# Attention on one core: fewer accumulating transfers in the softmax denominators, and their sums two key tiles earlier

## The chip, the cores and the metric

The kernel runs on one core of one Trainium2 chip. The metric is the device time of one execution in microseconds (us). The engines of the core are named as the profile names them: PE is TensorE (matmuls) and PEld its weight loads, DVE is VectorE, ACT is ScalarE, POOL is GpSimd, SP is SyncE, which here only issues transfers.

## What is computed

The reference is one transformer block, conditioned on a second input: batch 2, 2048 positions, width 512, 16 heads of 32, all in fp32.

```
h = _rmsnorm(x, g1) * (1.0 + scale1[:, None, :]) + shift1[:, None, :]
x = x + _mha(h, w_qkv, b_qkv, w_ao, b_ao, n_head)
h = _rmsnorm(x, g2) * (1.0 + scale2[:, None, :]) + shift2[:, None, :]
x = x + _ffn(h, w_fc, b_fc, w_fo, b_fo)

# in _mha:
attn = jnp.einsum('bhqd,bhkd->bhqk', q, k) * (1.0 / np.sqrt(hd))
attn = jax.nn.softmax(attn, axis=-1)
out = jnp.einsum('bhqk,bhkd->bhqd', attn, v)
```

The change touches only the softmax's denominators: for each head and query, the sum of the exponentials over all 2048 keys.

## The kernel before

Four stages follow each other: the weights' preparation, the projections of queries, keys and values (stage A), attention (stage B, `stage_b`), and the output projection with the feed-forward part. Stage B is where the change is.

Stage B works through 32 units. A unit is one group of 4 heads of one batch with one block of 512 queries; four units in a row share a group of heads, so keys and values are loaded once in four units. A unit has 16 key tiles (`NK`) of 128 keys, called kt 0 to 15. For each key tile and head TensorE makes a 128x512 block of scores (line 840, tile b_s, three banks used in turn), ScalarE exponentiates it into `pt` (line 696), and TensorE multiplies it with the values into b_o (line 895). `pt` is a ring of 8 slots, one key tile each with all 4 heads: key tile kt + 8 overwrites the slot of key tile kt. TensorE works two key tiles at a time: 16 matmuls of scores and of maxima (the next units' maxima, line 812, read by VectorE at line 756) and then the products of both key tiles, one group of 16 records at line 895. Scores run 3 blocks ahead of the products.

The denominators are made by two engines and the transfer engines. In unit u GpSimd first adds key tiles 0 and 1 into the accumulator `acc` (`first_pair`, line 719). Each other pair of key tiles, n = 0 to 6 for the key tiles 2n + 2 and 2n + 3, is first folded by an accumulating transfer of 1 MB, which adds the even slot into the odd one inside `pt` (`fold_pair`, line 726); it may start when the products of both have been made. Then GpSimd adds the odd slot into `acc` (`add_pair`, line 733). The slot of an even key tile is free for ScalarE when its transfer has landed, that of an odd one when its add is done; `slot_free` holds these waits. GpSimd has one instruction stream, written out by hand: while the transfer of pair n flies it adds pair n - 1. The last pair's add of unit u stands in unit u + 1, behind the first fold. When all of a unit's adds are done, four matmuls with a column of ones (`denominators`, line 819) sum `acc` over the partitions; they stand behind the products of key tile 7 of the next unit (`D_AT`), and ScalarE copies them out (line 668) at the place that `SUMS_AT` sets. SP issues, per unit, the loads of queries (768 KB), the store of the output (256 KB), small transfers for maxima and denominators, and in three of four units two or three loads of 512 KB of the next group's keys and values (`load_piece`; none from unit 28 on): one when the products of key tile 2 are done, one behind key tile 5, one behind the maxima.

Of the kernel before, what the change touches and what calls it, by code (L numbers as in the profile page):

```python
# [17 lines left out]
ALU = mybir.AluOpType  # L18
# [4 lines left out]
HD = D // H  # L23
# [6 lines left out]
GH = P // HD  # L30
NG = NB * H // GH
NK = T // P
UNITS = NG * NJ
# [438 lines left out]

PAIRS = NK // 2 - 1
ADDS = PAIRS + 1
RING = 8
LEAD = 3
EARLY = 4
TURN_AT = 3  # L480
SUMS_AT = 4 * 8 + LEAD


def score_place(i):

    return i + (i >= SUMS_AT)

# [6 lines left out]
def stage_b(nc, io, keep, scratch):  # L494
# [9 lines left out]
    with ExitStack() as stack:  # L504
        m = Memory(nc, stack, "b")
        ident, ones = keep["ident"], keep["ones"]
# [4 lines left out]
        pt = m.sb("pt", [P, RING, GH, TB])  # L511
        acc = [m.sb(f"acc{i}", [P, GH, TB]) for i in range(2)]
# [7 lines left out]
        ps_s, ps_m, ps_o = m.ps("s", LEAD), m.ps("m", EARLY), m.ps("o", 1)  # L520
        k_in, v_in, m_in = ([m.sem(f"{n}{i}") for i in range(2)] for n in ("k_in", "v_in", "m_in"))
        q_in = [m.sem(f"q_in{i}") for i in range(4)]
        pair_in = [m.sem(f"pair_in{i}") for i in range(2)]
# [13 lines left out]
        PER = ITEMS // NK  # L537
        AHEAD = PER * (NK - TURN)
        assert all(o.count("m") == PER and o.count("s") == GH for o in ORDER)
        D_AT = 7  # L540
        assert SUMS_AT == GH * (D_AT + 1) + LEAD

        def added(u, n):

            return ADDS * u + ADDS + (n + 3 if n < PAIRS - 1 else 2 + ADDS)

        STEPS = GH * NK
        assert ITEMS == STEPS
# [9 lines left out]
        def run(eng, body):  # L558
            for u in range(UNITS):
                body(u, u // 8, u % 8)  # L560
# [93 lines left out]
        @block.scalar  # L654
        def _(act):
            act.sem_inc(p_ready, STEPS)
            act.sem_inc(d_read, 1)

            def read_products(u):

                act.wait_ge(pv_done, NK * u + RING - 1)
                act.wait_ge(o_stored, 16 * (u + 1))
                act.activation(o_sb[:], ps_o[:, 0, :], ACT.Copy).then_inc(o_read, 1)

            def read_denominators(u):
                act.wait_ge(d_ps, u + 1 + 1)
                act.wait_ge(d_out, 16 * (u + 1))
                act.activation(d_sb[:], ps_s[:, SUMS_AT % LEAD, :], ACT.Copy).then_inc(d_read, 1)

            def slot_free(u, kt, pair, j):  # L670

                act.wait_ge(pv_done, NK * u + kt + 1)
                old = (kt - RING) % NK
                if old >= 2 and old % 2 == 0:
                    g = PAIRS * (j if kt >= RING else j - 1) + old // 2 - 1
                    if g >= 0:
                        act.wait_ge(pair_in[g % 2], 16 * (PAIRS * 4 * pair + g // 2 + 1 + g % 2))
                    else:
                        act.wait_ge(pool_added, added(u - 1, old // 2 - 1))
                elif old >= 2:  # L680
                    act.wait_ge(pool_added, added(u if kt >= RING else u - 1, old // 2 - 1))
                else:
                    act.wait_ge(pool_added, ADDS * u + ADDS + 1)

            act.wait_ge(ones_ready, 3)
            act.wait_ge(o_init, 1)

            def body(u, pair, j):
                for kt in range(NK):
                    slot_free(u, kt, pair, j)  # L690
                    for h in range(GH):
                        i = GH * kt + h
                        if i == SUMS_AT:
                            read_denominators(u)
                        act.wait_ge(st_done, STEPS * (u + 1) + i + 1)
                        act.activation(pt[:, kt % RING, h, :], ps_s[:, score_place(i) % LEAD, :], ACT.Exp,  # L696
                                       scale=SCALE).then_inc(p_ready, 1)
                        if i == GH:
                            read_products(u)

            run(act, body)
            read_products(UNITS)
            read_denominators(UNITS)

        @block.gpsimd
        def _(pool):
            pool.memset(one_rows, 1.0).then_inc(ones_ready, 1)
            pool.memset(acc[1][:], 1.0).then_inc(ones_ready, 1)
            pool.wait_ge(ones_in, 32)
            pool.memset(pt[:, RING - 2:RING, :, :], 1.0).then_inc(ones_ready, 1)  # L710
            pool.wait_ge(ones_ready, 3)
            pool.dma_start(pt[:, RING - 1, :, :], pt[:, RING - 2, :, :], accum_op=ALU.add).then_inc(pair_in[1], 16)
            pool.sem_inc(pool_added, ADDS)

            def first_pair(u, slot):

                pool.wait_ge(p_ready, STEPS * (u + 1) + GH * 2)
                pool.wait_ge(d_ps, u + 1)
                pool.tensor_tensor(acc[slot][:], pt[:, 0, :, :], pt[:, 1, :, :], ALU.add).then_inc(pool_added, 1)

            def fold_pair(u, j, pair, n):

                kt = 2 * n + 3
                pool.wait_ge(pv_done, NK * u + RING - 1 + kt + 1)
                pool.nop(nofuse=True)
                pool.dma_start(pt[:, kt % RING, :, :], pt[:, (kt - 1) % RING, :, :], accum_op=ALU.add).then_inc(pair_in[(PAIRS * j + n) % 2], 16)  # L726

            def add_pair(u, j, pair, n, slot):

                g = PAIRS * j + n  # L730
                pool.wait_ge(pair_in[g % 2], 16 * (PAIRS * 4 * pair + g // 2 + 1 + g % 2))
                pool.wait_ge(pool_added, added(u, n) - 1)
                pool.tensor_tensor(acc[slot][:], acc[slot][:], pt[:, (2 * n + 3) % RING, :, :], ALU.add).then_inc(pool_added, 1)  # L733

            def body(u, pair, j):
                first_pair(u, j % 2)
                fold_pair(u, j, pair, 0)
                add_pair(u - 1, j - 1, pair, PAIRS - 1, (j + 1) % 2)
                for n in range(1, PAIRS):
                    fold_pair(u, j, pair, n)  # L740
                    add_pair(u, j, pair, n - 1, j % 2)

            run(pool, body)
            pool.sem_inc(pool_added, 1)
            add_pair(UNITS - 1, 7, UNITS // 8 - 1, PAIRS - 1, 1)

        @block.vector
# [49 lines left out]
        def _(pe):  # L797
# [17 lines left out]
            def denominators(u, slot):  # L815

                pe.wait_ge(pool_added, added(u - 1, PAIRS - 1))
                for h in range(GH):
                    last = pe.matmul(ps_s[h * HD:(h + 1) * HD, SUMS_AT % LEAD, :], ones[:, 0:HD], acc[slot][:, h, :], start=True, stop=True)
                last.then_inc(d_ps, 1)  # L820

            def operands(j, pair):
# [8 lines left out]
            def scores(n, kslot, qslot, i):  # L831

                kt, h = i // GH, i % GH
                place = score_place(i)
                if place == SUMS_AT + LEAD:
                    pe.wait_ge(d_read, n + 2)
# [6 lines left out]
            for i in range(SUB):  # L843
                last = pe.matmul(ps_o[:, 0, i * P:(i + 1) * P], ones[:], ones[:], start=True, stop=True)
# [13 lines left out]
            def body(u, pair, j):  # L858
# [4 lines left out]
                for kt in range(NK):  # L863
# [28 lines left out]
                    for n in (kt - 1, kt):  # L892
# [4 lines left out]
                        last.then_inc(pv_done, 1)  # L897
                    if kt == D_AT:
                        pe.wait_ge(p_ready, STEPS * (u + 1) + SUMS_AT - LEAD + 1)
                        denominators(u, (j + 1) % 2)  # L900

            run(pe, body)
            denominators(UNITS, 1)


# [480 lines left out]
def build(nc, io, out):  # L1386

    scratch = {}
    for name, shape in (("qk_hi", (2, NG, P, T)), ("qk_lo", (2, NG, P, T)), ("v", (NG, P, NK, P)), ("o", (NG, P, T)),
                        ("h_hi", (NG, P, T)), ("h_lo", (NG, P, T)),   # L1390
                        ("y1", (NB, T, D)), ("m", (2, 2, GH * TB)), ("d", (GH, TB)), ("r", (NG, GH, T))):
        scratch[name] = nc.dram_tensor(f"scratch_{name}", shape, F32, kind="Internal").ap()
    with ExitStack() as whole:
        m = Memory(nc, whole, "keep")
        keep = {"chan": m.sb("chan", [P, C_ALL]), "cond_ab": m.sb("cond_ab", [P, NB, 4, KT]),
                "ident": m.sb("ident", [P, P]), "ones": m.sb("ones", [P, P]),
                "w_ao": m.both("w_ao", [P, KT, D])}
        with ExitStack() as early:
            m = Memory(nc, early, "early")
            keep |= {"w_hi": m.sb("w_hi", [P, KT, 3 * D], F32R), "w_lo": m.sb("w_lo", [P, KT, 3 * D], F32R),  # L1400
                     "cos": m.sb("cos", [P, T]), "sin": m.sb("sin", [P, T]), "bv": m.sb("bv", [P, D]),
                     "x": m.sb("x", [P, SUB, D])}
            stage_p(nc, io, keep)
            stage_a(nc, io, keep, scratch)
        nc.disable_value_cache = True
        stage_b(nc, io, keep, scratch)
        nc.disable_value_cache = False
        stage_cd(nc, io, keep, scratch, out)
# [43 lines left out]
```

## Time and profile before

| | us |
|---|---|
| median of 3 runs | 3324.93 (3324.06 to 3326.23) |
| profiled execution, its own time | 3321.67 |
| its span in the trace | 3319.9 |
| stage B from the first to the last regular group of sums | 508.02 to 2012.39 |

The span is from the first to the last instruction in the trace; the execution's own time is 1.8 us longer. Stage B has 33 groups of sums at line 819 (one for each unit and one of the start), and the distance from one to the next is the length of a unit. A unit is named below by the start of the group of sums that opens it.

### The profile page before, as it was taken

To read this page: it belongs to the slowest core of one execution; us is meant where nothing else is said; L and a number is where in the kernel's file an instruction comes from. 1 tells how busy PE (TensorE), PEld (TensorE's weight loads), DVE (VectorE), ACT (ScalarE), POOL (GpSimd) and SP (SyncE) were. 2 spreads that over 40 slices of the span, in tenths; PEclk is the share of its full clock that TensorE was granted. 3 is DMA by queue.
4 is the path that set the end of the run, shared out by engine and by line. 5 is a ranking of instruction groups with operands and counts; after the bars stand their busy time and mean duration, and the time that the engine had idled before them with its cause. 6 is when DMAs were issued, how large, how long until landed. Compare 5 with 4: busy or idle time off the path is not lost. (4 is left out here: it accounts for less than half of the span.)

```text
span 3319.9 us, 41114 instructions
## 1 busy us (share of the span) xinstructions
PE 3118.5 (94%) x15089; PEld 2089.3 (63%) x15089; DVE 1839.2 (55%) x2971; ACT 1513.8 (46%) x2790; POOL 1719.3 (52%) x748
## 2 busy tenths in 40 slices
PE   5999789999999999999999999399999999999999
PEld 5777545555555555555555553177888888888887
DVE  2566478787777787777887882153333333222222
ACT  1323117776666676676776776242222223111111
POOL 0445518888888888888888888432222310000000
PEclk9999859999999999999999999699999999999999
DMA  4454539899898998889999887522222211112110
GB/s 181 142 162 154 150 79 201 188 196 189 184 197 180 198 192 176 195 175 199 191 189 197 174 174 158 137 89 88 85 82 76 84 37 58 51 66 87 51 51 26
DMA packets 168670, 455.25 MB, mean 137 GB/s; under 512 B 23961, under 2 KB 57833, under 8 KB 135789
## 3 DMA queue, kind: packets, MB, share of 16 engines
q0 software_dynamic: 32400, 235.94, 35.6%
q1 hardware_dynamic: 134800, 211.01, 21.6%
q10 hardware_dynamic: 1296, 6.03, 0.5%
q8 instruction: 104, 1.70, 0.2%
q14 instruction: 70, 0.57, 0.1%
HBM read 137.94 MB, written 78.92 MB: 65 GB/s over the span
## 5 line engine op out<-in xcount | busy, mean ns | idle before, releaser
L756 DVE TENSOR_REDUCE b_mpart<-b_m 128x1 f32<-128x512 f32 x2048 | 1253.1, 681 | 342.4 <-PE b_m L812 341.8
L696 ACT ACTIVATE b_pt<-b_s 128x512 f32<-128x512 f32 x2048 | 1085.7, 603 | 418.5 <-PE b_s L840 358.5
L733 POOL TENSOR_TENSOR b_acc<-b_acc,b_pt 128x2048 f32<-128x2048 f32 x225 | 1045.9, 4648 | 207.8 <-DMA b_pt<-b_pt 205.4
L840 PE MATMUL b_s<-b_qs,b_ks 98*128 98x512 f32 x2048 | 856.7, 421 | 39.4 <-ACT b_pt L696 32.4
L812 PE MATMUL b_m<-b_ks,b_qs 96*128 96x512 f32 x2048 | 811.1, 423 | 20.3 <-issue 20.1
L840 PEld LDWEIGHTS b_s<-b_qs,b_ks 98*128 98x128 f32 x2048 | 390.0, 191 | 376.5 <-issue 183.6
L812 PEld LDWEIGHTS b_m<-b_ks,b_qs 96*128 96x128 f32 x2048 | 399.8, 195 | 173.0 <-DVE b_mpart L756 81.1
L895 PE MATMUL b_o<-b_pt,b_vg 128*32 128x512 f32 x4096 | 505.0, 611 | 0.0
L1212 DVE SCALAR_TENSOR_TENSOR e_u_lo_f<-e_a,keep_chan,e_u_lo_f 128x512 f32<-128x512 f32 x128 | 96.1, 751 | 547.9 <-PE e_a L1333 547.9
L1106 ACT ACTIVATE e_u_lo_f<-e_g,keep_chan 128x512 f32<-128x512 f32 x128 | 88.3, 690 | 423.6 <-PE e_g L1333 423.5
L895 PEld LDWEIGHTS b_o<-b_pt,b_vg 128*32 128x32 f32 x4096 | 108.5, 111 | 249.8 <-ACT b_pt L696 137.6
L1111 ACT ACTIVATE e_u_hi<-e_u_lo_f 128x512 fp32r<-128x512 f32 x128 | 81.0, 633 | 344.4 <-DVE e_u_lo_f L1212 344.4
L726 POOL DMA_DIRECT2D b_pt<-b_pt x224 | 204.6, 913 | 39.8 <-PE b_o L895 28.0
L1333 PE MATMUL e_g<-e_h_hi,e_w_hi 128*128 128x512 f32 x512 | 200.9, 392 | 13.1 <-DVE e_h_lo L1233 13.1
L1333 PE MATMUL e_a<-e_h_hi,e_w_hi 128*128 128x512 f32 x512 | 200.7, 392 | 0.0
L1343 PE MATMUL e_y<-e_w_hi,e_u_hi 128*128 128x512 f32 x512 | 200.7, 392 | 0.0
L1333 PE MATMUL e_g<-e_h_lo,e_w_hi 128*128 128x512 f32 x512 | 199.8, 390 | 0.0
L1333 PE MATMUL e_g<-e_h_hi,e_w_lo 128*128 128x512 f32 x512 | 199.8, 390 | 0.0
L1333 PE MATMUL e_a<-e_h_hi,e_w_lo 128*128 128x512 f32 x512 | 199.8, 390 | 0.0
L1343 PE MATMUL e_y<-e_w_hi,e_u_lo 128*128 128x512 f32 x512 | 199.7, 390 | 0.0
L1333 PE MATMUL e_a<-e_h_lo,e_w_hi 128*128 128x512 f32 x512 | 199.5, 390 | 0.0
L1343 PE MATMUL e_y<-e_w_lo,e_u_hi 128*128 128x512 f32 x512 | 199.5, 390 | 0.0
(140 smaller groups left out, 3300.3 us busy)
## 6 DMA issues: line engine op xcount, KB each, us to landing
b_pt<-b_pt POOLq DMA_DIRECT2D x225, 1024.0 KB, 8.2
scratch_qk_hi<-a_q_hi SPq DMA_DIRECT2D x64, 256.0 KB
scratch_qk_lo<-a_q_lo SPq DMA_DIRECT2D x64, 256.0 KB
b_qs<-scratch_qk_hi SPq DMA_DIRECT2D x64, 256.0 KB, 5.9
b_ks<-scratch_qk_hi SPq DMA_DIRECT2D x32, 512.0 KB, 7.0
scratch_o<-b_o_sb SPq DMA_DIRECT2D x33, 256.0 KB, 8.7
early_x<-in_x SPq DMA_DIRECT2D x8, 1024.0 KB, 8.2
scratch_v<-a_vsb SPq DMA_DIRECT2D x32, 256.0 KB, 4.4
```

The source lines that it names most:

```text
L696: act.activation(pt[:, kt % RING, h, :], ps_s[:, score_place(i) % LEAD, :], ACT.Exp, scale=SCALE).then_inc(p_ready, 1)
L726: pool.dma_start(pt[:, kt % RING, :, :], pt[:, (kt - 1) % RING, :, :], accum_op=ALU.add).then_inc(pair_in[(PAIRS * j + n) % 2], 16)
L733: pool.tensor_tensor(acc[slot][:], acc[slot][:], pt[:, (2 * n + 3) % RING, :, :], ALU.add).then_inc(pool_added, 1)
L756: dve.tensor_reduce(mpart[j % 2][:, i // 4, i % 4:i % 4 + 1], ps_m[:, at, :], AX.X, ALU.max).then_inc(max_done, 1)
L812: pe.matmul(ps_m[:, maximum_bank(j, place), :], qs[qslot][0:KR, h, s * P:(s + 1) * P], ks[kslot][0:KR, h, k * TB:(k + 1) * TB], start=True ...
L840: pe.matmul(ps_s[:, place % LEAD, :], ks[kslot][0:QR, h, kt * P:(kt + 1) * P], qs[qslot][0:QR, h, :], start=True, stop=True).then_inc(st_d ...
L895: last = pe.matmul(ps_o[h * HD:(h + 1) * HD, 0, :], vg[kslot][:, n, h * HD:(h + 1) * HD], pt[:, n % RING, h, :], start=n == 0, stop=n == N ...
L1106: act.activation(u_f[:, f % 2, :], ps_g[:, 0, :], ACT.Silu, bias=chan[:, t:t + 1]).then_inc(sg_ready, 1)
L1111: act.activation(u_hi[:, f % 2, :], u_f[:, f % 2, :], ACT.Copy).then_inc(uhi_ready, 1)
L1212: dve.scalar_tensor_tensor(u, ps_a[:, 0, :], chan[:, t:t + 1], u, ALU.add, ALU.mult).then_inc(uf_ready, 1)
L1333: last = pe.matmul(ps[:, 0, :], w[:, f, t, k, :], h[s][:, k, :], start=i == 0, stop=i == 3 * KT - 1)
L1343: last = pe.matmul(ps_y[:, i, :], u[:, f % 2, i * P:(i + 1) * P], w[:, f, :], start=f == 0 and n == 0, stop=f == NF - 1 and n == 2)
```

## The change

The last pair of a unit, key tiles 14 and 15, is no longer folded by a transfer. Key tile 14 is added by GpSimd straight from its slot (`add_single`), and key tile 15 by TensorE: the sums over the partitions take a second term, four more matmuls that read its slot and accumulate in the same bank. So a unit has six pairs (`PAIRS`) and six transfers, and still eight adds on GpSimd. The add of the last pair (key tiles 12 and 13) and the single add now stand ahead of `first_pair` of the next unit. The sums move from behind key tile 7 to behind key tile 5. The waits of the ring follow: the slot of key tile 14 waits for the single add, that of key tile 15 for the sums.

```
-PAIRS = NK // 2 - 1
-ADDS = PAIRS + 1
+PAIRS = NK // 2 - 2
+ADDS = PAIRS + 2
-SUMS_AT = 4 * 8 + LEAD
+SUMS_AT = 4 * 6 + LEAD
...
-        D_AT = 7
+        D_AT = 5
...
-            return ADDS * u + ADDS + (n + 3 if n < PAIRS - 1 else 2 + ADDS)
+            return ADDS * u + ADDS + (n + 4 if n < PAIRS - 1 else 2 + ADDS)
...
                 old = (kt - RING) % NK
-                if old >= 2 and old % 2 == 0:
+                if old == NK - 1:
+                    act.wait_ge(d_ps, u + 1 + 1)
+                elif old == NK - 2:
+                    act.wait_ge(pool_added, ADDS * u + ADDS + 1)
+                elif old >= 2 and old % 2 == 0:
...
-                else:
-                    act.wait_ge(pool_added, ADDS * u + ADDS + 1)
+                elif kt >= RING:
+                    act.wait_ge(pool_added, ADDS * u + ADDS + 3)
...
+            def add_single(u, slot):
+
+                pool.wait_ge(p_ready, STEPS * (u + 1) + GH * (NK - 1))
+                pool.wait_ge(pool_added, added(u, PAIRS - 2))
+                pool.tensor_tensor(acc[slot][:], acc[slot][:], pt[:, (NK - 2) % RING, :, :], ALU.add).then_inc(pool_added, 1)
+
             def body(u, pair, j):
+                add_single(u - 1, (j + 1) % 2)
+                add_pair(u - 1, j - 1, pair, PAIRS - 1, (j + 1) % 2)
                 first_pair(u, j % 2)
                 fold_pair(u, j, pair, 0)
-                add_pair(u - 1, j - 1, pair, PAIRS - 1, (j + 1) % 2)
                 for n in range(1, PAIRS):
                     fold_pair(u, j, pair, n)
                     add_pair(u, j, pair, n - 1, j % 2)
...
             def denominators(u, slot):
 
                 pe.wait_ge(pool_added, added(u - 1, PAIRS - 1))
-                for h in range(GH):
-                    last = pe.matmul(ps_s[h * HD:(h + 1) * HD, SUMS_AT % LEAD, :], ones[:, 0:HD], acc[slot][:, h, :], start=True, stop=True)
+                pe.wait_ge(p_ready, STEPS * (u + 1))
+                terms = [acc[slot][:]] + [pt[:, n % RING, :, :] for n in (NK - 1,)]
+                for n, term in enumerate(terms):
+                    for h in range(GH):
+                        last = pe.matmul(ps_s[h * HD:(h + 1) * HD, SUMS_AT % LEAD, :], ones[:, 0:HD], term[:, h, :],
+                                         start=n == 0, stop=n == len(terms) - 1)
                 last.then_inc(d_ps, 1)
```

GpSimd's stream around a unit's start, before: `first_pair` is line 719, the DMA rows are folds, and line 733 is `add_pair`. The piece runs from the last fold of a unit through the first two adds of the next.

```order
L726 DMA b_pt<-b_pt 128x2048
L733 TENSOR_TENSOR b_acc<-b_acc,b_pt 128x2048
L719 TENSOR_TENSOR b_acc<-b_pt 128x2048
L726 DMA b_pt<-b_pt 128x2048
L733 TENSOR_TENSOR b_acc<-b_acc,b_pt 128x2048
L726 DMA b_pt<-b_pt 128x2048
L733 TENSOR_TENSOR b_acc<-b_acc,b_pt 128x2048
```

The same place of the changed kernel, where line 730 is the fold, 737 `add_pair`, 743 `add_single` and 723 `first_pair`.

```order
L730 DMA b_pt<-b_pt 128x2048
L737 TENSOR_TENSOR b_acc<-b_acc,b_pt 128x2048
L743 TENSOR_TENSOR b_acc<-b_acc,b_pt 128x2048
L737 TENSOR_TENSOR b_acc<-b_acc,b_pt 128x2048
L723 TENSOR_TENSOR b_acc<-b_pt 128x2048
L730 DMA b_pt<-b_pt 128x2048 x2
L737 TENSOR_TENSOR b_acc<-b_acc,b_pt 128x2048
```

Ahead of `first_pair` there are now three adds in a row, and behind it two folds in a row with no add between them; before, the previous unit's last add stood between these two folds.

TensorE's stream at the sums of a unit, before, from the last products ahead of them.

```order
L895 MATMUL b_o<-b_pt,b_vg 32x512 x8
L819 MATMUL b_s<-b_acc,keep_ones 32x512 x4
L840 MATMUL b_s<-b_qs,b_ks 128x512
L812 MATMUL b_m<-b_ks,b_qs 128x512
```

And of the changed kernel, where it stands one group of products earlier (line 833 is the sums, 855 the scores, 823 the maxima, 910 the products).

```order
L910 MATMUL b_o<-b_pt,b_vg 32x512 x8
L833 MATMUL b_s<-b_acc,keep_ones 32x512 x4
L833 MATMUL b_s<-b_pt,keep_ones 32x512 x4
L855 MATMUL b_s<-b_qs,b_ks 128x512
L823 MATMUL b_m<-b_ks,b_qs 128x512
```

## Rows read from the trace of the kernel before

**Rows 1.** The page: busy time by engine, and slices of the span.
```profile
PE 3118.5 (94%) x15089; PEld 2089.3 (63%) x15089; DVE 1839.2 (55%) x2971; ACT 1513.8 (46%) x2790; POOL 1719.3 (52%) x748
...
POOL 0445518888888888888888888432222310000000
...
DMA  4454539899898998889999887522222211112110
```

**Rows 2.** Windows: stretch, length, busy us of PE, PEld, DVE, ACT, POOL, clock, DMA share, GB/s.
```profile
508.02:2012.39 1504.37, 1470.42 (x7954) 790.63 (x7950) 1196.03 (x2040) 1045.93 (x1980) 1273.91 (x451) 0.99 0.90 188
...
1058.46:1106.89 48.43, 48.35 (x269) 26.25 (x265) 39.80 (x68) 34.84 (x66) 42.13 (x16) 1.00 0.90 188
1106.89:1160.54 53.65, 50.26 (x270) 26.50 (x266) 40.08 (x68) 34.92 (x66) 42.32 (x16) 0.97 0.95 196
```

**Rows 3.** Waits of ACT between 556.5 and 2012.4: total, times, longest.
```profile
ACT b_pt L696 <- POOL b_acc L733: 39.8, 17, 4.4
ACT b_pt L696 <- DMA b_pt<-b_pt: 9.6, 7, 3.1
```

**Rows 4.** Timeline of PE around the sums, and one unit's products.
```profile
1058.46 1.04 PE L819 MATMUL b_s<-b_acc,keep_ones 128*32 128x512 f32 x8
1059.43 0.50 PE L840 MATMUL b_s<-b_qs,b_ks 98*128 98x512 f32 x1
...
1093.49 1.92 PE L895 MATMUL b_o<-b_pt,b_vg 128*32 128x512 f32 x16
...
1099.31 1.92 PE L895 MATMUL b_o<-b_pt,b_vg 128*32 128x512 f32 x16
...
1105.15 1.92 PE L895 MATMUL b_o<-b_pt,b_vg 128*32 128x512 f32 x16
```

**Rows 5.** Timeline of POOL, an undisturbed unit.
```profile
1042.26 4.59 POOL L719 TENSOR_TENSOR b_acc<-b_pt 128x2048 f32<-128x2048 f32 x1
1047.57 0.87 POOL L726 DMA_DIRECT2D b_pt<-b_pt  x1 [0.73 <-PE b_o L895]
1048.18 4.86 POOL L733 TENSOR_TENSOR b_acc<-b_acc,b_pt 128x2048 f32<-128x2048 f32 x1
1053.38 0.87 POOL L726 DMA_DIRECT2D b_pt<-b_pt  x1 [0.33 <-POOL b_acc L733]
1054.62 4.58 POOL L733 TENSOR_TENSOR b_acc<-b_acc,b_pt 128x2048 f32<-128x2048 f32 x1 [0.37 <-DMA b_pt<-b_pt]
...
1072.24 0.87 POOL L726 DMA_DIRECT2D b_pt<-b_pt  x1 [0.83 <-PE b_o L895]
...
1080.01 4.57 POOL L733 TENSOR_TENSOR b_acc<-b_acc,b_pt 128x2048 f32<-128x2048 f32 x1 [1.07 <-DMA b_pt<-b_pt]
```

**Rows 6.** Timeline of POOL, the next unit, with loads of keys.
```profile
1101.81 0.88 POOL L726 DMA_DIRECT2D b_pt<-b_pt  x1 [0.32 <-POOL b_acc L733]
...
1112.26 4.59 POOL L733 TENSOR_TENSOR b_acc<-b_acc,b_pt 128x2048 f32<-128x2048 f32 x1 [3.18 <-DMA b_pt<-b_pt]
...
1122.27 0.87 POOL L726 DMA_DIRECT2D b_pt<-b_pt  x1
...
1132.09 4.59 POOL L733 TENSOR_TENSOR b_acc<-b_acc,b_pt 128x2048 f32<-128x2048 f32 x1 [0.96 <-PE b_o L895]
```

**Rows 7.** Timeline of ACT: exponentials of an undisturbed unit, then of the disturbed one.
```profile
1053.27 4.24 ACT L696 ACTIVATE b_pt<-b_s 128x512 f32<-128x512 f32 x8 [1.58 <-PE b_s L840]
...
1150.10 2.06 ACT L696 ACTIVATE b_pt<-b_s 128x512 f32<-128x512 f32 x4 [3.07 <-DMA b_pt<-b_pt]
1154.73 3.26 ACT L696 ACTIVATE b_pt<-b_s 128x512 f32<-128x512 f32 x6 [2.56 <-POOL b_acc L733]
```

**Rows 8.** All folds (L726) between 556.5 and 2012.4.
```profile
DMA to landing us min/median/max: 6.9/8.3/13.4
```

**Rows 9.** Timeline of POOL, last unit: its first fold and its last add.
```profile
2050.88 0.87 POOL L726 DMA_DIRECT2D b_pt<-b_pt  x1 [1.43 <-PE b_o L895]
...
2093.96 4.49 POOL L733 TENSOR_TENSOR b_acc<-b_acc,b_pt 128x2048 f32<-128x2048 f32 x1 [1.49 <-DMA b_pt<-b_pt]
```

More of the change, by code:

```diff
@@ L709, in _ @@
             pool.wait_ge(ones_in, 32)
-            pool.memset(pt[:, RING - 2:RING, :, :], 1.0).then_inc(ones_ready, 1)
+            pool.memset(pt[:, RING - 4:RING, :, :], 1.0).then_inc(ones_ready, 1)
             pool.wait_ge(ones_ready, 3)
-            pool.dma_start(pt[:, RING - 1, :, :], pt[:, RING - 2, :, :], accum_op=ALU.add).then_inc(pair_in[1], 16)
+            pool.dma_start(pt[:, RING - 3, :, :], pt[:, RING - 4, :, :], accum_op=ALU.add).then_inc(pair_in[1], 16)
             pool.sem_inc(pool_added, ADDS)
@@ L743, in _ @@
             run(pool, body)
-            pool.sem_inc(pool_added, 1)
+            add_single(UNITS - 1, 1)
             add_pair(UNITS - 1, 7, UNITS // 8 - 1, PAIRS - 1, 1)
```

## The prediction, made before the changed kernel had run

> **What bounds the kernel now.** I read the page's busy times and slices first. TensorE is busy 94% of the span, and GpSimd, busy over half of it, has its work in stage B alone, where the transfer engines run at 8 to 9 tenths as well [rows 1]. So stage B has three nearly full resources, and the average doesn't say which one ends a unit. The windows do. The 30 units from 508.02 to 2012.39 took 1504.37 us, 50.15 each, but an undisturbed one takes 48.43 us with PE busy for 48.35 and a clock of 1.00, and a disturbed one 53.65 at 0.97 [rows 2]. The floor of a unit is thus TensorE's 48.43 us, and 1504.37 - 30 x 48.43 = 51.5 us are stalls on top.
>
> The waits name their cause: ScalarE waited 39.8 us for GpSimd's adds and 9.6 us for the accumulating transfers, 49.4 us together [rows 3], always for a slot of the ring. In the disturbed unit both stand next to each other [rows 7]: the transfer and the add of the unit's last pair were late, and with the exponentials the scores, since TensorE has three banks for them.
>
> **GpSimd's chain.** Call the start of a unit's first products 0. From the sums at 1058.46, which follow the start of the products of key tile 7 by 1.74 us (1105.15 to 1106.89), and from groups 5.83 us apart [rows 2, 4], the undisturbed unit has its 0 at 1039.23 and the next at 1087.66. A fold starts 2.5 us behind its group of products (1053.38 against 1050.88). An add takes 4.58 us, the next add starts 0.6 us behind a fold's issue (1047.57 to 1048.18), and the first transfer's add starts 7.05 us after its issue, the fifth's 7.77 [rows 5]. Call that time D. The last pair's add ends at 1053.04, and key tile 7's first exponential, second in the batch of 1053.27, starts at 1053.87 [rows 5, 7]: 0.8 us in hand. With loads beside them D is longer: 10.45 for the second transfer, 9.82 for the fifth [rows 6]; the median to landing is 8.3, the shortest 6.9 [rows 8].
>
> When GpSimd is late and no product holds a fold back, fold n + 2 follows add n, and add n waits for landing n. Its unit is then a loop through every second transfer: D, add 0 (fold 2 follows), D, add 2, D, add 4, then fold 6's issue, add 5 and the next first_pair. That is 3D + 3 x 4.58 + 0.6 + 4.58 + 4.59 = 3D + 23.5. At D = 8.3 it is 48.4, the very floor of TensorE. This explains why some units stall and some don't.
>
> **The change, part by part.**
>
> TensorE. Four more matmuls with the column of ones, of the same shape as those at line 819, which took 1.04 us, the next instruction starting 0.97 us after them [rows 4]. I take 0.97; half a group of products (1.92 for eight) gives 0.96, so no range is needed. All of it lies on TensorE, which nothing covers in an undisturbed unit: the floor becomes 49.40 us. Over 32 units that is +31 us. Moving the sums two key tiles up costs nothing by itself: what they wait for, the last add of the unit before, comes earlier too (below). The new wait for exponentials of the unit before is long fulfilled, and ScalarE's wait for the sums before it writes key tile 7 stands right behind its own copy of these sums.
>
> Transfers. One of seven goes, 1 MB of some 9 MB a unit. GpSimd saves its issue (0.87, of which 0.6 lay in the loop). Its adds stay eight: the single add takes the place of the seventh pair's.
>
> GpSimd's order. The loop is now D, add 0, D, add 2, D, add 4, single add, add 5, first_pair: 3D + 5 x 4.58 + 4.59 = 3D + 27.5, four us more for the same D. The reason: before, the last add of the previous unit stood between folds 0 and 1, inside the first flight; now the two folds stand next to each other, and GpSimd has nothing to do until transfer 0 has landed, 6 us or more. The second fold can't help, as it also waits for the products of key tile 5 (11.65 + 2.5 = 14.15). The loop equals the floor of 49.40 only at D = 7.3, against 8.3 before.
>
> What is due when. The last transferred pair is key tiles 12 and 13, and key tile 5 overwrites slot 13. This exponential lies as far behind the products of key tile 3 as key tile 7's did behind those of key tile 5 (1053.87 - 1050.88 = 3.0): 5.83 + 3.0 = 8.8. In an undisturbed unit fold 4 starts 1087.66 - 1072.24 = 15.4 us before the next 0, its add after 7.77, and three adds end at -15.4 + 7.8 + 13.7 = 6.1. So 2.7 us are in hand where 0.8 were. But they are in hand once: with D above 7.3 each unit eats 3 x (D - 7.3), and none gives back, since even undisturbed transfers are near 7.3.
>
> Which D. It can't be below 6.9, the shortest seen, and has little reason to lie above 8.3, the median with a seventh transfer in the way. For relief: the seventh transfer flew beside the query loads into the next unit's first. Against: when GpSimd is late, folds 0 and 1 go out at 13 to 14, just as SP's load behind key tile 5 does in three of four units; that load now strikes transfer 0, which is in the loop, and not transfer 1 alone. The load behind the maxima still meets transfers 3 and 4. With 8.5, 7.4 and 8.1 for transfers 0, 2 and 4 I take a mean D of 8.0: a loop of 51.5 us, 2.1 above the floor, in the 28 units that have or follow such loads.
>
> In sentences of its own, a page's price: the Trainium skill, DMA: Bandwidth & Descriptors, Anatomy of one DMA, gives a transfer from GpSimd 2.0 us plus its bytes over 436 GB/s, an estimate of 4.4 us for 1 MB. By it the loop would be 40.7 us and TensorE would bind every unit. The rows show no landing below 6.9 for these accumulating transfers, so I go by the rows.
>
> The sum: TensorE +31; the old stalls, -51.5; the new ones, 28 x 2.1 less the 2.7 in hand, +56; the end of the last unit, where TensorE is done and only the chain counts: before 47.6 us from its first fold to the end of its last add (2050.88 to 2098.45 [rows 9]), now 3 x 7.3 + 5 x 4.58 = 44.8, -3. Together +32.5. The longer filling of two more slots at the start lies ahead of the first exponential and has no reader that waits. The profiled execution took 3321.67, giving 3354; the median of the runs is 3.3 above it, giving 3358.
>
> **The rivals.**
>
> No stalls at all (0.20). One transfer less and the queries' loads falling between units bring D to 7.3 or less; the 2.7 us in hand take up the rest. For it: D was 7.05 where nothing else flew. Against: the loads haven't changed. It gives +31 - 51.5 - 3 = -23.5, 3301. This is the case on the other side; it decides from D = 7.3.
>
> Break-even (0.13). A D of 7.65 makes a loop of 50.45, stalls of 28 x 1.05 - 2.7 = 27, and a sum of +3: 3328.
>
> Worse (0.17). The two folds in a row and the load beside them leave D at 8.3 or raise it. At 8.3: 52.4, stalls 81, +57.5: 3382. At 8.5: 53.0, stalls 98, +74.5: 3399. For it also: stalls of some us took the clock to 0.97 [rows 2], though a TensorE that waits for GpSimd anyway loses little by that. The same Trainium skill page, Queues, rings and completion order, says that the engines take turns between queues packet by packet, by which a load beside transfer 0 would delay it by as much as its own bytes. That the second transfer took 10.45 beside a load [rows 6] agrees.
>
> **How the numbers follow.** My forecast, D between 7.7 and 8.3 (3332 to 3382), has 0.50. The range over all cases, from just below the stall-free case to between 8.3 and 8.5, is 3300 to 3394. A measurement tells some 0.2% of this kernel, 6.6 us, from no change. Faster is the first rival, 0.20; same the second, 0.13; slower the rest, 0.67.
>
> **What would show it.** TensorE: sums of 16 records, 2.0 us, and a shortest unit near 49.4. GpSimd: a wait of 5 us or more between the second fold and the first add of each unit, three adds and first_pair without a gap. ScalarE: its waits for line 737 before the exponentials of key tile 5, more than 49 us in total, and none for the single add. If the mean unit is at 49.4 and D below 7.3, the first rival holds. If key tile 5 doesn't wait and units are still long, the chain is not what I read, and my forecast is wrong in its cause too.

## The result: slower, and the profile after

The changed kernel took 3386.77 us (median of 4 runs, 3383.93 to 3398.74) where the kernel before took 3324.49 in the same comparison. The ratio is 1.0197, with a 95% interval of 1.0169 to 1.0224: slower by 62 us. The forecast was 3358, in a range of 3300 to 3394, with 0.67 on slower. Every time and ratio here is of fast executions; one execution of a later kernel, at 3903.26 us with a granted clock of 0.75, is left out.

The windows of the kernel after, with the columns of [rows 2]: all 30 regular units, an undisturbed one and a disturbed one.

```profile
500.23:2065.58 1565.35, 1515.57 (x8195) 804.55 (x8191) 1197.47 (x2040) 1047.53 (x1980) 1247.05 (x419) 0.98 0.77 160
1077.82:1127.13 49.31, 49.23 (x277) 26.54 (x273) 39.78 (x68) 34.76 (x66) 41.67 (x15) 1.00 0.79 162
1127.13:1182.35 55.22, 51.83 (x279) 27.61 (x274) 40.06 (x68) 35.07 (x66) 42.56 (x16) 0.94 0.79 168
```

The mean unit is 52.18 us (1565.35 / 30) where it was 50.15. The floor, an undisturbed unit, is 49.31 where it was 48.43 [rows 2]. So TensorE's part is 0.88 us a unit, and the stalls are 2.87 a unit, 86 us in 30 units, where they were 51.5. The share of the transfer engines fell from 0.90 to 0.77 and GpSimd's busy time fell by 27 us over these 30 units, and yet the units are longer: neither total is what binds.

TensorE at the sums of the undisturbed unit, then ScalarE's waits for GpSimd and the transfers between 556.5 and 2050 (us in total, times, longest), and the folds' time to landing.

```profile
1077.82 1.04 PE L833 MATMUL b_s<-b_acc,keep_ones 128*32 128x512 f32 x8
1078.68 1.04 PE L833 MATMUL b_s<-b_pt,keep_ones 128*32 128x512 f32 x8
1079.65 0.50 PE L855 MATMUL b_s<-b_qs,b_ks 98*128 98x512 f32 x1
```

```profile
ACT b_pt L700 <- POOL b_acc L737: 68.6, 34, 4.8
ACT b_pt L700 <- DMA b_pt<-b_pt: 10.7, 11, 2.1
```

```profile
DMA to landing us min/median/max: 7.0/8.5/14.7
```

The next score starts 1.83 us after the sums, against 0.97 in [rows 4]. ScalarE waits 79.3 us where it waited 49.4 [rows 3], in 34 places for an add where it was 17. None of the waits is for the single add of line 743. The median landing of all folds is 8.5 where it was 8.3 [rows 8], with one transfer in seven gone.

GpSimd's timeline around the start of the disturbed unit, up to the same place of the next.

```profile
1118.15 4.59 POOL L737 TENSOR_TENSOR b_acc<-b_acc,b_pt 128x2048 f32<-128x2048 f32 x1
1122.70 4.60 POOL L723 TENSOR_TENSOR b_acc<-b_pt 128x2048 f32<-128x2048 f32 x1
1127.25 1.74 POOL L730 DMA_DIRECT2D b_pt<-b_pt  x2
1136.40 4.58 POOL L737 TENSOR_TENSOR b_acc<-b_acc,b_pt 128x2048 f32<-128x2048 f32 x1 [7.42 <-DMA b_pt<-b_pt]
1140.93 0.86 POOL L730 DMA_DIRECT2D b_pt<-b_pt  x1
1141.54 4.89 POOL L737 TENSOR_TENSOR b_acc<-b_acc,b_pt 128x2048 f32<-128x2048 f32 x1
1146.07 1.20 POOL L730 DMA_DIRECT2D b_pt<-b_pt  x1
1149.50 4.57 POOL L737 TENSOR_TENSOR b_acc<-b_acc,b_pt 128x2048 f32<-128x2048 f32 x1 [2.23 <-DMA b_pt<-b_pt]
1154.02 0.88 POOL L730 DMA_DIRECT2D b_pt<-b_pt  x1
...
1161.65 4.58 POOL L737 TENSOR_TENSOR b_acc<-b_acc,b_pt 128x2048 f32<-128x2048 f32 x1 [0.91 <-DMA b_pt<-b_pt]
1166.38 4.60 POOL L743 TENSOR_TENSOR b_acc<-b_acc,b_pt 128x2048 f32<-128x2048 f32 x1
1171.12 4.54 POOL L737 TENSOR_TENSOR b_acc<-b_acc,b_pt 128x2048 f32<-128x2048 f32 x1
1175.62 4.53 POOL L723 TENSOR_TENSOR b_acc<-b_pt 128x2048 f32<-128x2048 f32 x1
1180.09 0.88 POOL L730 DMA_DIRECT2D b_pt<-b_pt  x1
```

This is the loop as the prediction wrote it. The two folds of 1127.25 stand side by side and GpSimd is idle for 7.42 us. From this fold to the next unit's first are 52.84 us: the flights of transfers 0, 2 and 4 to their adds are 9.15, 8.57 and 7.63, together 25.35, and 27.5 more is 52.85. Near its end, at 1175.74, ScalarE starts the exponential of key tile 5 on the end of the add of 1171.12.

```profile
1171.41 0.60 ACT L700 ACTIVATE b_pt<-b_s 128x512 f32<-128x512 f32 x1 [1.00 <-PE b_s L855]
1175.74 2.08 ACT L700 ACTIVATE b_pt<-b_s 128x512 f32<-128x512 f32 x4 [3.73 <-POOL b_acc L737]
```

The unit itself is longer than this loop, 55.22 us. TensorE stood still for 3.15 us before that exponential freed it, and from then to the sums it was granted a clock of 0.56:

```profile
1176.40:1182.30 5.90, 5.90 (x23) 2.86 (x27) 2.08 (x3) 3.21 (x6) 4.58 (x2) 0.56 0.20 42
```

This puts the sums 2.3 us later behind the exponential than in the unit before (6.6 us against 4.3), and it isn't added to the total: the next unit takes 51.1 us, 2.4 less than its own loop.

**All units, not one.** These means are worked out from GpSimd's timelines: for each of the first 30 units, from the issue of transfer n to the start of its add. The loop is the sum of the flights of transfers 0, 2 and 4 plus the steps outside them: 23.5 us before, 27.5 after. The last three columns are in us per unit.

| kernel | transfer 0 | 1 | 2 | 4 | loop | measured unit | shortest unit |
|---|---|---|---|---|---|---|---|
| before | 8.20 | 9.37 | 7.79 | 8.72 | 48.2 | 50.15 | 48.4 |
| changed | 8.40 | 12.35 | 7.66 | 8.59 | 52.15 | 52.18 | 49.3 |

In the changed kernel the mean loop is the mean unit. And the three flights in the loop add up to the same in both kernels, 24.71 and 24.65 us: what grew is the part outside them. Only transfer 1 flies longer, and it isn't in the loop.

### The profile page after: what moved, and what is told of

Read it like the earlier page. It is cut to its first block and busy times, and to the rows that moved or that the text cites. A ratio compares the mean times of both kernels' runs of the same rounds, so it can differ in the third digit from the quotient of the medians.

```text
span 3382.9 us, 41580 instructions
## 1 busy us (share of the span) xinstructions
PE 3164.1 (94%) x15353; PEld 2104.5 (62%) x15353; DVE 1841.6 (54%) x2971; ACT 1515.6 (45%) x2790; POOL 1697.6 (50%) x717
## 5 line engine op out<-in xcount | busy, mean ns | idle before, releaser
L737 POOL TENSOR_TENSOR b_acc<-b_acc,b_pt 128x2048 f32<-128x2048 f32 x193 | 892.6, 4625 | 294.0 <-DMA b_pt<-b_pt 288.5
L730 POOL DMA_DIRECT2D b_pt<-b_pt x192 | 173.4, 916 | 45.8 <-PE b_o L910 45.4
```

## Experiments

The theory is the prediction's: the order of GpSimd's stream costs 4 us of loop a unit, because no add lies in the first flight. Rivals are TensorE's added matmuls, the earlier deadline of the sums, GpSimd's amount of work, and the flights themselves. Each ratio below is to the kernel before in the same comparison (3321.56 us for experiments 1, 3 and the first kernel of 4, 3322.65 for the others). The changed kernel's own ratio is the 1.0197 above; it was not run again beside them.

**1. The first fold ahead of first_pair.**

```
             def body(u, pair, j):
                 add_single(u - 1, (j + 1) % 2)
                 add_pair(u - 1, j - 1, pair, PAIRS - 1, (j + 1) % 2)
-                first_pair(u, j % 2)
                 fold_pair(u, j, pair, 0)
+                first_pair(u, j % 2)
```

> The changed kernel with the first fold of a unit issued ahead of first_pair instead of behind it, nothing else. Theory (the order of GpSimd's stream is the cost): the loop through every second transfer falls from 3D + 27.5 to 3D + 22.9, since first_pair now runs inside the first flight. At the D of 8.5 measured in the changed kernel (median to landing) that is 48.4 us a unit, under TensorE's 49.3, so only units with loads stall a little: mean unit 49.4 to 49.9, total 3303 to 3320, faster than both. Rival (TensorE's four extra matmuls and the earlier deadline are the cost): the order of two GpSimd steps changes nothing, 3380 to 3390.

Measured: 3309.58 us, ratio 0.9959 (0.9946 to 0.9972), faster than both kernels and 77 us below the changed one. The window of the 30 regular units, and GpSimd's timeline at a unit's start in this kernel:

```profile
502.99:1994.20 1491.21, 1479.60 (x8194) 794.53 (x8190) 1194.18 (x2040) 1046.20 (x1980) 1255.27 (x421) 1.00 0.81 169
```

```profile
1088.01 4.61 POOL L737 TENSOR_TENSOR b_acc<-b_acc,b_pt 128x2048 f32<-128x2048 f32 x1
1095.11 0.88 POOL L730 DMA_DIRECT2D b_pt<-b_pt  x1 [2.50 <-PE b_o L910]
1095.72 4.90 POOL L723 TENSOR_TENSOR b_acc<-b_pt 128x2048 f32<-128x2048 f32 x1
1100.92 0.87 POOL L730 DMA_DIRECT2D b_pt<-b_pt  x1 [0.30 <-POOL b_acc L723]
1102.81 4.60 POOL L737 TENSOR_TENSOR b_acc<-b_acc,b_pt 128x2048 f32<-128x2048 f32 x1 [1.01 <-DMA b_pt<-b_pt]
```

Now GpSimd waits 2.50 us for TensorE's products ahead of the fold, which is the sign that it is on time, and 1.01 us for the transfer where it waited 7.42 us. The mean unit is 49.71 us (1491.21 / 30), 0.4 above the floor, at a clock of 1.00. ScalarE's waits for adds, and the folds' landing:

```profile
ACT b_pt L700 <- POOL b_acc L737: 5.9, 5, 1.5
```

```profile
DMA to landing us min/median/max: 7.0/7.8/11.5
```

The same work on every engine and the same transfers, in another order on one engine: the rival that TensorE's matmuls or the earlier deadline are the cost is out. The landings are shorter too. The flight of transfer 0 to its add, over all units, fell from a mean of 8.3 to 7.75 us, which I had not counted on: the load of keys or values behind key tile 5 is now issued 4.7 to 5.3 us after this fold, where in the changed kernel it mostly came 0.1 to 3.8 us after it. That gives 0.5 us a unit; the rest of the shorter loop is the 4.6 us of the add.

**2. An add more, where GpSimd had the gap.**

```
+            def extra(u, slot):
+                pool.wait_ge(p_ready, STEPS * (u + 1) + GH * 2)
+                pool.wait_ge(d_ps, u + 1)
+                pool.tensor_tensor(acc[slot][:], pt[:, 0, :, :], pt[:, 1, :, :], ALU.add).then_inc(extra_done, 1)
...
+                pool.wait_ge(extra_done, u + 1)
...
-                first_pair(u, j % 2)
+                extra(u, j % 2)
                 fold_pair(u, j, pair, 0)
+                first_pair(u, j % 2)
```

> The changed kernel with the sum of key tiles 0 and 1 made twice by GpSimd, once ahead of the first fold (where the changed kernel has it) and once behind it (where the fold-first kernel has it): nine adds a unit instead of eight, the output unchanged. Theory: the second one lies in the first flight, where GpSimd only waited, so the loop stays 3D + 27.5 and the time that of the changed kernel, 3380 to 3395; it also says that the fold-first kernel's gain comes back when an add stands ahead of the fold. Rival (GpSimd is bound by its work, and order matters only through it): 32 x 4.6 = 147 us more in total, up to 3530.

Measured: 3386.96 us, ratio 1.0192 (1.0173 to 1.0211), which can't be told from the changed kernel's 1.0197 (3386.96 and 3386.77 us), with 146 us more of GpSimd work, as the page's busy row says (1697.6 us in the changed kernel):

```profile
PE 3165.0 (93%) x15353; PEld 2099.2 (62%) x15353; DVE 1840.1 (54%) x2971; ACT 1515.2 (45%) x2790; POOL 1844.0 (54%) x749
```

Its timeline around the fold, in which line 731 is the add ahead and 725 the one behind:

```profile
1122.16 4.61 POOL L731 TENSOR_TENSOR b_acc<-b_pt 128x2048 f32<-128x2048 f32 x1
1126.70 0.87 POOL L738 DMA_DIRECT2D b_pt<-b_pt  x1
1127.31 4.91 POOL L725 TENSOR_TENSOR b_acc<-b_pt 128x2048 f32<-128x2048 f32 x1
...
1136.23 4.57 POOL L745 TENSOR_TENSOR b_acc<-b_acc,b_pt 128x2048 f32<-128x2048 f32 x1 [3.19 <-DMA b_pt<-b_pt]
```

An add behind the fold is free, and an add ahead of it is in the loop with its whole 4.6 us. Not all of that reaches the time: the mean unit goes from 49.71 to 52.30 us, 2.6 more, because the shorter loop lay under TensorE's floor. This pair of experiments settles the cause: the second kernel is the first with one add put back ahead of the fold, and 77 us come back with it. The same measures as above, with 22.9 and 27.5 us outside the flights:

| kernel | transfer 0 | 1 | 2 | 4 | loop | measured unit | shortest unit |
|---|---|---|---|---|---|---|---|
| fold first | 7.77 | 9.42 | 7.82 | 8.54 | 47.0 | 49.71 | 49.3 |
| add more | 8.41 | 9.40 | 7.71 | 8.66 | 52.3 | 52.30 | 49.3 |

GpSimd's amount of work is out as a rival. So is the thought that two folds in a row are the cost: here they are 5.1 us apart, transfer 1 flies 9.4 us instead of 12.35, and the time is the same.

**3. TensorE's part, twice.** In the changed kernel the accumulator is summed once more as a third term, which leaves the denominators wrong by that part. In the kernel before, the sums are made twice, which doubles the denominators.

```
-                terms = [acc[slot][:]] + [pt[:, n % RING, :, :] for n in (NK - 1,)]
+                terms = [acc[slot][:]] + [pt[:, n % RING, :, :] for n in (NK - 1,)] + [acc[slot][:]]
```

```
+                for n in range(2):
                     for h in range(GH):
-                    last = pe.matmul(..., acc[slot][:, h, :], start=True, stop=True)
+                        last = pe.matmul(..., acc[slot][:, h, :], start=n == 0, stop=n == 1)
```

> The changed kernel with a third term in the sums (the accumulator once more, so the denominators are wrong by that part): the price of four matmuls doubled. Theory: only the units near the floor of 49.3 us pay the 0.96 us, about 13 of 30, in the stalled ones the wait behind it shrinks: +10 to +16 us, about 3399. Rival (TensorE's work is what the change cost): every unit pays, +31 us, 3417.

> The kernel before with the sums made twice (four more matmuls, the accumulator as second term, so the denominators are doubled): TensorE's part of the change alone. Theory: the floor rises from 48.4 to 49.4 us, but the stalls shrink by what the chain catches up meanwhile: +15 to +22 us, about 3343. Rival (all of it adds up): +31 us, 3356.

Measured: 3392.27 us for the third term, ratio 1.0218 (1.0192 to 1.0244), which can't be told from the changed kernel's 1.0197, though 10 to 16 us were expected; and 3329.76 us for the double sums, ratio 1.0018 (1.0002 to 1.0035), 8 us above the kernel before, where 15 to 22 were expected. Both are less than I expected, and far from the 31 us of the rival. With the third term the 30 units take as long as the changed kernel's 1565.35 us, though the shortest unit rose to 50.1: its loop, 52.1 us by its flights, was already over the floor, so TensorE's work hides behind it.

```profile
501.93:2067.27 1565.34, 1526.35 (x8434) 806.47 (x8430) 1196.56 (x2040) 1046.33 (x1980) 1248.35 (x420) 0.99 0.77 160
```

The 13 units near the floor, which I had expected to pay for the matmuls, were mostly catching up with a loop that ran behind. In the kernel before, the sums of the double-sum kernel are also 49.3 us apart in an undisturbed unit, so all of the 0.88 us shows where nothing stalls; but a longer unit of TensorE gives GpSimd's loop time to catch up, and the stalls of the 30 units shrink by nearly as much, from 51.5 to 28 us. ScalarE's waits for adds fell from 39.8 us [rows 3] to 22.6 in this kernel:

```profile
ACT b_pt L696 <- POOL b_acc L733: 22.6, 14, 4.3
```

**4. A load moved away from the first two folds.**

```
-                sp.wait_ge(pv_done, NK * u + RING - 1 + 6)
-                if nG < NG:
-                    load_piece(j, nG, ni, 1)
                 spread_denominators(u)
+                sp.wait_ge(pv_done, NK * u + RING - 1 + 10)
+                if nG < NG:
+                    load_piece(j, nG, ni, 1)
```

> The changed kernel with SP's second load of keys or values (512 KB, three of four units) moved from behind key tile 5 to behind key tile 9, so that it no longer flies beside the first two folds. Theory: the loop's length depends on the sum of the flights of transfers 0, 2 and 4; the first gets shorter (8.4 to about 7.6 us to its add), but the load now meets transfer 2 or 3: -10 to +5 us, 3377 to 3392. Rival (the collision of this load with transfer 0 is the main cost): -20 us or more, below 3367.

Measured: 3375.47 us, ratio 1.0155 (1.0131 to 1.0180), about 11 us less than the changed kernel (14 by the ratios). That is just below the theory's 3377 to 3392 and well short of the rival's 3367. Transfer 0 now has its add 7.1 us after its issue (median), 1.1 us less in the mean of 30 units; transfers 2, 3 and 4 take 0.4, 1.0 and 0.3 us more, and the median landing is 8.4. So the load beside transfer 0 was a part of D, as forecast, and two thirds of it only move within the loop. The loop by its flights is 51.8 us, the measured unit 51.88. On top of the fold-first kernel the same edit does nothing:

> Both edits together: the first fold ahead of first_pair, and SP's second load of keys or values behind key tile 9 instead of 5. The fold-first kernel ran at a mean unit of 49.7 us against a floor of 49.3, so at most 12 us are left. Theory: the load later gives back little or nothing where the loop is already under the floor: 0.9940 to 0.9970 of before. Rival (loads beside folds cost by themselves): it goes on gaining as it did in the changed kernel, 12 us, below 0.9935.

Measured: 3311.75 us, ratio 0.9964 (0.9950 to 0.9977), against 0.9959 without it, though the three flights of the loop are 0.6 us shorter together. Once the loop is under the floor, a shorter flight is worth nothing, as the theory had it.

**5. Loads cut to an eighth.** In both kernels, from the third group of heads on, so that those groups' attention is made with old keys and values.

```
-                sp.dma_start(f32(ks[i][r * HD:(r + 1) * HD, heads, :]), src[1, G][:, heads, :]).then_inc(k_in[i], 16)
+                n = T if G < 2 else T // 8
+                sp.dma_start(f32(ks[i][r * HD:(r + 1) * HD, heads, 0:n]), src[1, G][:, heads, 0:n]).then_inc(k_in[i], 16)
...
-                part = slice(NK // 2 * half, NK // 2 * (half + 1))
+                part = slice(NK // 2 * half, NK // 2 * (half + 1) if G < 2 else NK // 2 * half + 1)
```

> The changed kernel with the loads of the next group's keys and values cut to an eighth (64 KB instead of 512 KB) from the third group on, so in 24 of the 28 units with loads; the attention of those groups then uses old keys and values. Theory: with less beside them the flights of transfers 0, 2 and 4 come near 7.3 us, the loop near the floor of 49.3 us: most of 86 us of stalls goes, 3310 to 3335. Rival (what delays the transfers is their own neighbours, two folds in a row): D stays above 8, no more than 20 us gained, above 3365.

> The kernel before with the same cut of the loads. Theory: its loop of 3D + 23.5 is 45.4 us at a D of 7.3, well under 48.4, so nearly all of its 51.5 us of stalls goes: 3278 to 3292. The difference to the changed kernel without loads is then about the 31 us of TensorE's matmuls and what the loop of 49.4 adds. Rival (the stalls have another cause than the loads): no more than 15 us gained.

Measured: the changed kernel 3329.18 us, ratio 1.0017 (1.0005 to 1.0030), 58 us less; the kernel before 3279.87 us, ratio 0.9872 (0.9852 to 0.9893), 43 us less. Both are in the theory's ranges: most of the stalls, 43 of 51.5 us and 58 of 86, come from flights that loads lengthen. The waits of ScalarE for adds, and the folds' landing, of the kernel before with small loads (first) and the changed one:

```profile
ACT b_pt L697 <- POOL b_acc L734: 14.2, 6, 4.3
```

```profile
ACT b_pt L701 <- POOL b_acc L738: 32.2, 25, 4.8
```

```profile
DMA to landing us min/median/max: 6.9/7.6/13.3
```

```profile
DMA to landing us min/median/max: 7.0/7.7/14.2
```

The landings are nearly the same and the waits are not, 6 against 25: the mean flight of transfers 0, 2 and 4 to their adds is 7.6 us in both. There the loop of 3D + 23.5 is 46.3 us, under a floor of 48.4, and the mean unit is 48.8; that of 3D + 27.5 is 50.3, over a floor of 49.3, and the mean unit is 50.5. This is the difference of the two loops seen at one D, and why the changed kernel keeps a third of its stalls even with small loads.

## Why the prediction was right, point by point

The direction and the mechanism were right: a longer loop of GpSimd, from its order. The size was not. The profiled execution grew by 63 us where 32.5 were forecast, and 3387 us lies outside the 3332 to 3382 that had 0.50, in the territory of the third rival (0.17). That the whole range held it says little, since it ran from a kernel without stalls to one worse than my own case.

- **The floor.** TensorE's added part was taken at 0.97 us, a floor of 49.40. It measured 0.88, a floor of 49.31: the second term of the sums starts 0.86 us after the first.
- **GpSimd's loop, 3D + 27.5.** Shown: 52.84 us in the disturbed unit against 52.85 by the formula, over 30 units the formula gives a mean of 52.15 us, and the mean unit is 52.18. That an add ahead of the first fold is part of it is shown by experiments 1 and 2, which take out one add and put it back.
- **What is late, and where.** Shown: key tile 5 waits for the add of key tiles 12 and 13, nothing waits for the single add, and ScalarE's waits grew over 49 us. The disturbed unit shown had a clock of 0.94, the one of the kernel before 0.97 [rows 2]. That did not add to the total, as the rival thought it might: the unit behind made it up, and the mean unit is the mean loop.
- **The size of D.** Taken were 8.5, 7.4 and 8.1 for transfers 0, 2 and 4. Over the 30 units the means are 8.40, 7.66 and 8.59: 24.65 instead of 24.0, a loop of 52.15 instead of 51.5. Transfer 0 was judged rightly; transfer 4 took 0.5 us more than I gave it, and the reason was not tested.
- **The sum of stalls.** This is the term that was mis-sized: forecast +56 us, measured 86. The flights explain 18 of the 30 (28 x 0.65). All 30 units follow the loop, and not 28, which is 6 more. The floor of 49.31 instead of 49.40 makes 2.5 (and takes 3 from TensorE's +31). The 2.7 us in hand brought nothing on balance: GpSimd did fall 5.2 us further behind TensorE over these units, but it also spent 6 us in its loop waiting for products. Undisturbed units of 49.3 us don't contradict this, they catch up with a GpSimd that runs behind.
- **The old stalls.** Taking away the measured 51.5 us was right, but the mean loop doesn't explain them: it is 48.2 us before, under the floor of 48.43. There single units with long flights stall, and the others can't run below the floor to give it back. That reading is argued from the units' lengths (48.4 to 55.5 us) and not tested by itself; experiment 5, which shortened the flights and took 43 us away, agrees.
- **The end of the last unit.** Forecast 44.8 us from its first fold to the end of its last add, against 47.6 before. In the kernel after, these rows make it 44.6 (2115.21 to 2159.82):

```profile
2115.21 0.88 POOL L730 DMA_DIRECT2D b_pt<-b_pt  x1
...
2155.33 4.49 POOL L737 TENSOR_TENSOR b_acc<-b_acc,b_pt 128x2048 f32<-128x2048 f32 x1
```

- **The rivals.** That the stalls vanish was wrong because D did not fall with one transfer less: the flights in the loop are 24.65 us together where they were 24.71. The two folds in a row lengthened transfer 1 alone, which costs nothing (experiment 2), so this reason of the third rival was wrong too, although its 3382 was nearer than my own case. The order in experiment 1 made the first rival's forecast (3301) nearly come true, by a shorter loop more than by a shorter D.

The Trainium skill's price for a transfer (DMA: Bandwidth & Descriptors, Anatomy of one DMA), from which the estimate of 4.4 us came, was left aside for the rows, and the measurement decides: no landing of these accumulating transfers was below 6.9 us in any kernel, not even with the loads cut. The Trainium skill also says that the engines take turns between queues packet by packet (the same page, Queues, rings and completion order). Transfer 0 taking 9.15 us to its add with a load of keys issued 0.1 us behind it fits that, and so do the 7.1 us without the load in experiment 4; no run here shows the turns themselves.

## What to carry to other kernels

When one engine both issues transfers and does the work that waits for them, write its unit down as a loop: which transfer's flight lies in it, and which steps stand inside a flight. A step that moves from inside a flight to ahead of the issue lengthens the loop by its whole length even if the engine's busy time falls. What the program pays is what then stands above the other engines' floor, and taking work off two busy resources (here the transfers and GpSimd) gains nothing if the loop through both gets longer. Check with the mean over all units: if it equals the mean loop, work on any other engine hides behind it, as the third term of experiment 3 did. Issue the transfer first and do the independent step behind it: here that one swap turned 1.0197 into 0.9959.

## What was not expected of the hardware

In 12 of 32 units of the changed kernel the two folds were issued 0.6 to 0.7 us apart, and the second had its add 11.7 to 14.8 us after its issue; in the kernel before, where they are 5.1 to 6.4 us apart, it was 7.1 to 11.0. The first was not slower for it: transfer 0 takes 8.40 us to its add in the changed kernel and 8.41 in the one with an add more, whose folds are 5.1 us apart or more. And 146 us of additional GpSimd work, running while transfers were in flight, left the three flights of the loop at 24.8 us together against 24.65, the median landing between 556 and 2000 at 8.5, and the time unchanged.
